# Five row groups of 256, 384, 512, 512 and 384 in place of four of 512, and a shorter free run of gathers, in a recommendation tower

## Chip, core and metric

The kernel runs on one core of one Trainium2 chip. The metric is the device time of one execution in microseconds (us). Engines are named as the profile names them: PE is TensorE (PEld its weight loads), DVE is VectorE, ACT is ScalarE, POOL is GpSimd, SP is SyncE, which here only issues DMAs.

## What is computed

2,048 rows, 40 table fields, embeddings of 64 values. Each row gathers 40 embeddings by index. For each of the 780 field pairs (i, j) with i < j a 64 x 64 matrix W is applied to embedding i and the result is multiplied with embedding j and summed. The 780 sums and 16 dense values go through three dense layers (512, 256, 1).

```python
e = jnp.stack([tbl_0[ids[:, 0]], ..., tbl_39[ids[:, 39]]], axis=1)
viW = jnp.einsum('bpd,pde->bpe', e[:, i_idx, :], W)
z = jnp.einsum('bpe,bpe->bp', viW, e[:, j_idx, :])
h = jnp.concatenate([z, dense_ctx], axis=1)
h = jnp.maximum(h @ W_top1 + b_top1, 0.0)
h = jnp.maximum(h @ W_top2 + b_top2, 0.0)
y = h @ W_top3
```

All values are fp32.

## The kernel before

The 2,048 rows are worked on in groups (`SIZES`, four of 512). A group has 128-row tiles (`TILES`, four each). The 40 fields form 20 pairs; pair m of a group (m = 0 to 19) holds fields 2(19 - m) and 2(19 - m) + 1, so the highest fields come first.

**Gathers (POOL, L459).** One indirect DMA fetches one field for one tile of 128 rows, so a pair takes 2 x TILES gathers: 8 in every group, 160 a group, 640 in all. The first four pairs of a group go to `VN` (two buffers, by group), the other sixteen to a ring `stage` of four pairs. Before pair m POOL waits until the pair four places before it in the ring has been transposed (L445, `tr_before`), and before the first pair of group g > 1 until group g - 2 is through the multiplies (L444). In group 0 the gathers run freely behind each other; from pair `RUN_PAIRS` = 4 on, every second tile is preceded by a "rest", a memset of a scratch tile (L456) that POOL waits for. In groups 1 to 3 each gather has a mark, computed ahead by `schedule`: it waits for a given count of PE steps (L451), or, where the mark is None, does a rest.

**Units (PE, DVE, ACT).** A transpose step turns a pair around on PE (L606) and ACT copies it to `V` (L489). Row k of a group is the work of field pair k with all higher ones; it needs pair m = 19 - k and those before it, so rows run from k = 19 down to 0. A group has 136 "a" and "d" units, whose matmuls (L624) stream the group's rows (512 columns), and B_ROWS x TILES = 64 "b" units, whose matmuls (L620) stream 512 columns of weights for one tile of 128 rows, whatever the group's size. Every unit has 16 matmul instructions and one DVE multiply (L564 for a and d, L555 for b). Two a or d units share one reduction step on PE (L644, 16 matmuls, 68 steps a group, streaming the group's rows). The b products are summed by ACT (L477, 16 pairs of instructions a unit) or, for some units, by DVE (L539). At the end of a group come one transpose step of those sums (L653), two passes over `z` (L494, L573, L501, L507) and seven MLP steps (L665 four times, L672 twice, L678), which are spread over the next group's units; those of the last group stand at its end.

**Order.** PE, ACT and DVE follow orders computed before the kernel is built. `schedule` keeps a clock of its own (`now`, `STEP_US`, `GATHER_US`, `REST_US`, `LAND_US`) to order the transposes among the steps and to place the gather marks: one gather each time its variable `due` has passed, and `due` then moves on by `SPACE_US`.

**Weights (SP, L430).** W is loaded in chunks of 640 KB into three slots, 22 chunks a group, in each group again.

Of the kernel before, what the change touches and what calls it, by code (L numbers as in the profile page):

```python
# [5 lines left out]
B, F, D, DENSE = 2048, 40, 64, 16  # L6
N1, N2 = 512, 256
P128 = 128
SIZES = (512, 512, 512, 512)
GROUPS = len(SIZES)  # L10
GB = max(SIZES)
FIRST_ROW = [sum(SIZES[:_g]) for _g in range(GROUPS)]
TILES = [_s // P128 for _s in SIZES]
PAIRS = F // 2
JP = 4
J0 = PAIRS - JP
CROWD = 11
# [4 lines left out]
def row_items(k):  # L22

    last = J0 if k < B_ROWS else PAIRS
    out = [("b", k)] if k < B_ROWS else []
    out += [("a", k, jp) for jp in range(last - 1, k, -1)]
    return out + ([("d", k)] if k % 2 == 0 else [])  # L30


def group_units(g):

    a_items = [item for k in reversed(range(PAIRS)) for item in row_items(k) if item[0] != "b"]
    b_items = [("b", k, t) for k in reversed(range(B_ROWS)) for t in range(TILES[g])]
    out, i, last = [], 0, 0  # L40
    for a, item in enumerate(a_items):
        out.append(item)
        coming = a_items[a + 1][1] if a + 1 < len(a_items) else -1
        while i < len(b_items):
            k = b_items[i][1]
            if g == 0 and not (k >= item[1] or k > coming):
                break
            if a < (3 + 1.94 * i if g else last if k >= CROWD else last + 2):
                break
            out.append(b_items[i])  # L50
            i, last = i + 1, a
    return out
# [4 lines left out]
UNITS = [(_g, _u) for _g in range(GROUPS) for _u in GROUP_UNITS[_g]]  # L57
# [111 lines left out]
def gathers(m):  # L169


    return 2 * TILES[m // PAIRS]
# [16 lines left out]
               if x % PAIRS >= JP and (stage_index(m) - stage_index(x)) % STAGE_SLOTS == 0)  # L189


RUN_PAIRS = 4
MLP_APART = 24


def red_at(q):


    late = 1.9 if q % QUADS == PART_ENDS[0] else 0
    return min(A_AT[2 * q + 1] + LAG + 0.1 + late, TOTAL - 0.4 + 0.0001 * q)  # L200


def ztr_at(g):


    return B_AT[B0[g + 1] - 1] + 7.2


def mlp_at(g, m):


    at = red_at((g + 1) * QUADS - 1)
    return at + 0.01 * (m + 1) if g == GROUPS - 1 else int(at) + 12.6 + MLP_APART * m


def pair_needed(step):


    return step[1] * PAIRS + PAIRS - 1 - UNITS[step[2]][1][1]


def tr_before(m):


    before = stage_index(m) - STAGE_SLOTS
    if m % PAIRS < JP or before < 0:
        return 0
    return before // (PAIRS - JP) * PAIRS + before % (PAIRS - JP) + JP + 1


def stage_free(m, transposed):
    return transposed >= tr_before(m) and (m % PAIRS or m < 2 * PAIRS or transposed >= 0)


STEP_US = {"main": 0.885, "red": 0.885, "tr": 0.65, "ztr": 1.0}
GATHER_US, REST_US, LAND_US, SPACE_US = 1.25, 0.55, 6.0, 1.6


def step_us(step):
    if step[0] == "mlp":  # L240
        return 6.15 if step[2] < 4 else 3.6 if step[2] < 6 else 1.8
    return STEP_US[step[0]]


def schedule():

    steps = [(n, ("main", UNITS[n][0], n)) for n in range(TOTAL)]  # L250
    steps += [(red_at(q), ("red", *divmod(q, QUADS))) for q in range(GROUPS * QUADS)]
    steps += [(ztr_at(g), ("ztr", g, 0)) for g in range(GROUPS)]
    steps += [(mlp_at(g, m), ("mlp", g, m)) for g in range(GROUPS) for m in range(MLP_STEPS)]
    steps = [s for _, s in sorted(steps, key=lambda x: x[0])]
    landed, end = {}, 8.0
    for m in range(PAIRS):
        end += gathers(m) * GATHER_US + (TILES[0] // 2 * REST_US if m >= RUN_PAIRS else 0)
        landed[m] = end + 2.2
    out, marks, count, now, due, pair = [], [], {"main": 0, "red": 0, "mlp": 0, "ztr": 0}, 0.0, end, 0
    issued = PAIRS  # L260
    for at, step in enumerate(steps):
        if step[0] == "main":
            need = pair_needed(step)
            while pair <= need:
                now = max(now, landed[pair]) + STEP_US["tr"] + (1.3 if pair == need else 0)
                out.append(("tr", *divmod(pair, PAIRS)))
                pair += 1
        if pair < issued and landed[pair] <= now and (pair < 2 * PAIRS or count["main"] >= U0[pair // PAIRS - 1] + 4):
            out.append(("tr", *divmod(pair, PAIRS)))
            now += STEP_US["tr"]  # L270
            pair += 1
        out.append(step)
        now += step_us(step)
        count[step[0]] += 1
        room = int(step_us(steps[at + 1]) / 1.9) if at + 1 < len(steps) else 0
        if due > now + (0.9 if room > 1 else 0):
            continue
        for extra in range(max(room, 1)):
            if issued == GROUPS * PAIRS or step[0] == "ztr" or not stage_free(issued, pair):
                break  # L280
            marks.append(None if extra else (step[0], count[step[0]]))
            if extra + 1 >= room:
                due = max(now + 1.9 * extra - 1.0, due) + SPACE_US
            if len(marks) == sum(gathers(m) for m in range(PAIRS, issued + 1)):
                landed[issued] = now + 1.9 * extra + LAND_US
                issued += 1
    return out, marks
# [30 lines left out]
def z0_tile(g):  # L318


    return ZT if g % 2 else 0
# [6 lines left out]
def build(nc, ids, tables, dense_t, w_units, w1, b1, w2, b2, w3, y):  # L328
# [6 lines left out]
    with ctx:  # L335
        def sb(name, shape, dt=fp32):
            return ctx.enter_context(nc.sbuf_tensor(name, shape, dt))
# [18 lines left out]
        idx = sb("idx", [P128, B // P128, F], i32)  # L356
        ident = sb("ident", [P128, P128])
        sel = sb("sel", [P128, 63])
        rest = sb("rest", [P128, 256])

        Ups = ctx.enter_context(nc.psum_tensor("Ups", [P128, U_SLOTS, 2, 512], fp32))
        Zps = ctx.enter_context(nc.psum_tensor("Zps", [P128, 2, 512], fp32))
# [29 lines left out]
        def wait(eng, s, value):  # L392
            if value > 0:
                eng.wait_ge(s, value)

        def natural_rows(m, t):


            g, r = divmod(m, PAIRS)
            if r < JP:  # L400
                at = P128 * (JP - 1 - r)
                return VN[:, g % 2, t, at:at + P128]
            return stage[:, stage_index(m) % STAGE_SLOTS, t, :]

        def landed(m):
            r = m % PAIRS
            return natural[r] if r < JP else gathered[stage_index(m) % STAGE_SLOTS]

        @block.sync
        def _(sp):  # L410
            sp.dma_start(idx[:, :, :], ids).then_inc(idx_loaded, 16)
            for c, (group, load) in enumerate(CHUNKS):
# [11 lines left out]
                for g in range(GROUPS):  # L424
                    if c == w_of(J_LAST[g])[0] + 4:
                        sp.wait_ge(z0_done, g + 1)
                        sp.dma_start(z[DENSE_ROW:DENSE_ROW + DENSE, z0_tile(g), :SIZES[g]],
                                     dense_t[:, FIRST_ROW[g]:FIRST_ROW[g] + SIZES[g]]).then_inc(dense_loaded, 16)
                x = W_SETS[min(group, 1)] + load
# [4 lines left out]
        @block.gpsimd  # L434
        def _(pool):
            pool.memset(ident[:, :], 0.0).then_inc(ident_zeroed, 1)
            pool.wait_ge(ident_zeroed, 1)
            pool.affine_select(out=ident[:, :], in_=ident[:, :], compare_op=ALU.not_equal, fill=1.0, base=0,
                               pattern=[[-1, P128]], channel_multiplier=1).then_inc(ident_ready, 1)
            pool.wait_ge(idx_loaded, 16)  # L440
            pool.wait_ge(ident_ready, 1)
            marks, rests = iter(GATHER_MARKS), 0
            for m in range(GROUPS * PAIRS):
                g, r = divmod(m, PAIRS)  # L444
                if r == 0 and g > 1:  # L445
                    pool.wait_ge(mul_done, U0[g - 1])
                wait(pool, tr_done, tr_before(m))
                for t in range(TILES[g]):
                    for f in range(2):
                        mark = next(marks) if g else None  # L450
                        if mark:  # L451
                            kind, count = mark
                            pool.wait_ge({"main": main_done, "red": red_done, "mlp": mlp_done}[kind], count)
                        elif g or m >= RUN_PAIRS and f == 0 and t % 2 == 0:
                            rests += 1
                            pool.memset(rest[:, :], 0.0).then_inc(rested, 1)  # L456
                            pool.wait_ge(rested, rests)
                        field = 2 * (PAIRS - 1 - r) + f
                        pool.indirect_dma_start(  # L459
                            out=natural_rows(m, t)[:, D * f:D * f + D], out_offset=None, in_=tables[field][:, :],  # L460
                            in_offset=bass.IndirectOffsetOnAxis(
                                ap=idx[:, FIRST_ROW[g] // P128 + t, field:field + 1], axis=0),
                        ).then_inc(landed(m), 16)
# [272 lines left out]
```

## Time and profile before

| | us |
|---|---|
| Median of 3 runs | 1421.53 (1421.38 to 1423.5) |
| Profiled execution, its own time | 1418.47 |
| Profiled execution, span | 1416.7 |
| PE busy | 1265.5 (89%) |
| DVE busy | 989.6 (70%) |
| ACT busy | 880.7 (62%) |
| POOL busy | 624.0 (44%) |
| DMA, mean over 16 engines | 60 GB/s |

The span runs from the first to the last instruction of the profiled execution; the execution's own time is 1.8 us longer. An engine's busy time is the union of its instructions' times. In the windows below "(x647)" is the number of instructions that began in the window; for POOL that counts gathers and rests together.

### The profile page before, as it was taken

The page shows a single profiled execution, that of the slowest core. Times are in us where ns is not written, and L with a number is a line of the kernel's source. Part 1 is how long each engine was busy: PE and PEld are TensorE (multiplying, and loading weights), DVE is VectorE, ACT ScalarE, POOL GpSimd, SP SyncE. Part 2 cuts the span into 40 slices and gives each one's busy share as a digit, 9 for nine tenths or more (in the row PEclk, how much of TensorE's full clock was granted, in tenths as well). Part 3 has the DMA queues.
Part 4 walks back from the last instruction along what each step waited for, and adds up shares of the span by engine and source line. Part 5 has one row for each costly group of instructions (what it writes and reads, how often), then busy time and mean ns, then how long its engine had stood idle before and what let it go on. Part 6 is the DMA issues. An engine that isn't in the chain of part 4 may idle for free.

```text
span 1416.7 us, 46045 instructions
## 1 busy us (share of the span) xinstructions
PE 1265.5 (89%) x17808; PEld 483.8 (34%) x17808; DVE 989.6 (70%) x855; ACT 880.7 (62%) x6749; POOL 624.0 (44%) x700
## 2 busy tenths in 40 slices
PE   1027788999999999999999999999999999999999
PEld 0011122233343443333333434343334333333333
DVE  0024554557898787778888777878888777799990
ACT  0004444546756387668786577778875677788871
POOL 6735344431355555555555555555555555100000
PEclk9998889999999999999999999999999999999999
DMA  4102111111222222222222222222232122212200
GB/s 154 25 16 54 32 53 34 52 50 45 69 59 77 76 62 57 75 56 77 57 76 68 68 77 58 75 51 68 71 79 77 39 78 57 65 40 60 75 21 0
DMA packets 34752, 84.45 MB, mean 60 GB/s; under 512 B 12196, under 2 KB 12708, under 8 KB 34408
## 3 DMA queue, kind: packets, MB, share of 16 engines
q1 hardware_dynamic: 14048, 60.50, 13.9%
q0 software_dynamic: 20480, 21.01, 7.5%
q8 instruction: 142, 2.33, 0.7%
q14 instruction: 74, 0.61, 0.1%
q10 hardware_dynamic: 8, 0.01, 0.0%
HBM read 81.47 MB, written 0.01 MB: 58 GB/s over the span
## 4 chain that ended last, share of the span: by engine, by line
PE 68%; issue 10%; DVE 9%; another core or an unknown queue 8%; ACT 4%; DVEq 0%
PE Ups L624 29%; PE Ups L620 14%; PE Zps L644 13%; PE Ups L665 7%; DVE P L564 6%; ACT PB L477 3%; DVE PB L555 2%; PE Ups L672 2%; PE Ups L606 2%; DVE zB L539 1%; PE Ups L678 0%; PE Ups L653 0%; ACT V L489 0%; ACT L489 0%
## 5 line engine op out<-in xcount | busy, mean ns | idle before, releaser
L477 ACT ACTIVATE PB<-PB 128x64 f32<-128x64 f32 x3312 | 798.7, 250 | 257.9 <-DVE PB L555 223.4
L564 DVE TENSOR_TENSOR P<-Ups,V 128x1024 f32<-128x1024 f32 x544 | 650.7, 1220 | 276.9 <-remote 153.1
L624 PE MATMUL Ups<-V,wf 64*32 64x512 f32 x8704 | 661.3, 602 | 100.9 <-ACT V L489 63.9
L477 ACT ACTIVATION_READ_ACCUMULATOR PB<-PB 128x1 f32 x3312 | 648.0, 196 | 0.5 <-issue 0.5
L459 POOL DMA_INDIRECT stage<-tbl,idx x512 | 484.6, 947 | 345.0 <-PE Ups L624 161.1
L555 DVE TENSOR_TENSOR PB<-Ups,VN 128x1024 f32<-128x1024 f32 x256 | 311.8, 1220 | 113.1 <-PE Ups L620 64.2
L620 PE MATMUL Ups<-wf,V 64*32 64x512 f32 x4096 | 347.5, 607 | 14.2 <-issue 6.6
L644 PE MATMUL Zps<-P,sel 64*32 64x512 f32 x4352 | 342.2, 596 | 2.0 <-issue 1.1
L624 PEld LDWEIGHTS Ups<-V,wf 64*32 64x32 f32 x8704 | 191.1, 107 | 420.1 <-issue 189.7
L459 POOL DMA_INDIRECT VN<-tbl,idx x128 | 121.2, 947 | 133.8 <-PE Ups L624 78.3
L620 PEld LDWEIGHTS Ups<-wf,V 64*32 64x32 f32 x4096 | 98.6, 108 | 181.9 <-issue 116.3
L644 PEld LDWEIGHTS Zps<-P,sel 64*32 64x32 f32 x4352 | 111.1, 108 | 144.4 <-issue 132.3
L489 ACT COPY V<-Ups 128x512 f32<-128x512 f32 x80 | 46.1, 576 | 134.9 <-remote 66.5
L665 PE MATMUL Ups<-z,w1s 128*128 128x512 f32 x224 | 99.6, 598 | 0.0
L456 POOL MEMSET rest<- 128x256 f32 x54 | 17.6, 325 | 112.1 <-PE Ups L606 112.1
L665 PEld LDWEIGHTS Ups<-z,w1s 128*128 128x128 f32 x224 | 41.5, 190 | 58.2 <-issue 50.5
L539 DVE TENSOR_REDUCE zB<-PB 128x16 f32<-128x1024 f32 x49 | 59.3, 1210 | 0.0
L515 ACT ACTIVATE h<-Ups,b1s 128x512 f32<-128x512 f32 x16 | 11.0, 689 | 77.0 <-PE Ups L665 77.0
L606 PEld LDWEIGHTS Ups<-ident,stage 128*128 128x128 f32 x256 | 27.9, 142 | 54.8 <-issue 23.0
L606 PE MATMUL Ups<-ident,stage 128*128 128x128 f32 x256 | 42.7, 290 | 2.1 <-DVE P L564 1.0
L606 PE MATMUL Ups<-ident,VN 128*128 128x128 f32 x64 | 11.8, 312 | 29.2 <-DMA VN<-tbl,idx 28.9
L672 PE MATMUL Ups<-h,w2s 128*128 128x512 f32 x64 | 29.2, 602 | 0.6 <-DVE P L564 0.6
(21 smaller groups left out, 63.0 us busy)
## 6 DMA issues: line engine op xcount, KB each, us to landing
wf<-w_units SPq DMA_DIRECT2D x88, 640.0 KB
stage<-tbl,idx POOLq DMA_INDIRECT x512
VN<-tbl,idx POOLq DMA_INDIRECT x128
w1s<-w SPq DMA_DIRECT2D x1, 1792.0 KB
w2s<-w SPq DMA_DIRECT2D x1, 512.0 KB
idx<-ids SPq DMA_DIRECT2D x1, 320.0 KB, 3.0
z<-dense_t SPq DMA_DIRECT2D x4, 32.0 KB
y<-z ACTq DMA_DIRECT2D x4, 2.0 KB
```

The costliest lines, as they stand in the source:

```text
L459: pool.indirect_dma_start(out=natural_rows(m, t)[:, D * f:D * f + D], out_offset=None, in_=tables[field][:, :], in_offset=bass.IndirectOff ...
L477: last = act.activation(p, p, ACT.Copy, accum_out=zB[:, t, at:at + 1])
L489: act.copy(V[:, v_slot(g, PAIRS - 1 - x), :rows], Ups[:, slot, 0, :rows]).then_inc(v_done, 1)
L539: dve.tensor_reduce(zB[:, t, at:at + 4 * JP], PB[:, i % PB_SLOTS, :, :].rearrange("p b (j e) -> p (b j) e", e=D), AX.X, ALU.add).then_inc( ...
L555: dve.tensor_tensor(PB[:, B_INDEX[n] % PB_SLOTS, :, :], Ups[:, slot, :, :], v, ALU.mult).then_inc(mul_done, 1)
L564: dve.tensor_tensor(P[:, A_INDEX[n] % P_SLOTS, :, :rows], Ups[:, slot, :, :rows], v, ALU.mult).then_inc(mul_done, 1)
L606: last = pe.transpose(Ups[:, slot, 0, P128 * t:P128 * (t + 1)], natural_rows(m, t), ident[:, :])
L620: last = pe.matmul(Ups[out, slot, b, :], V[rows, v_slot(g, k), r0:r0 + 32], wf[rows, c % W_SLOTS, at:at + WB_COLS], start=True, stop=True)
L624: last = pe.matmul(Ups[out, slot, b, :size], wf[rows, c % W_SLOTS, at + 32 * strip:at + 32 * strip + 32], V[rows, v_slot(g, field), :size] ...
L644: last = pe.matmul(Zps[out, h, :size], sel[rows, 31 - to:63 - to], P[rows, a % P_SLOTS, strip % 2, :size], start=at == 0, stop=x + 1 == PA ...
L665: last = pe.matmul(Ups[:, slot, 0, :size], w1s[:, k % ZT, P128 * x:P128 * (x + 1)], z[:, k, :size], start=n == 0, stop=n == ZT - 1)
L672: last = pe.matmul(Ups[:, slot, 0, :size], w2s[:, k, P128 * (x - 4):P128 * (x - 3)], h1[:, k, :size], start=k == 0, stop=k == 3)
```

## The change

The group sizes become 256, 384, 512, 512 and 384, so `TILES` is 2, 3, 4, 4, 3 and the groups have 4, 6, 8, 8 and 6 gathers a pair. A matmul of an a or d unit, of a reduction, a transpose copy and an MLP step then streams 256 or 384 columns in the smaller groups; a b unit stays as it is, and there are 16 x TILES of them. In group 0 only the first 14 pairs (56 gathers) are issued in the free run, with one rest before each pair from the fifth on (`QUIET_PAIRS` = 4); its last six pairs (24 gathers) and all of groups 1 to 4 have marks. The rest tile has 512 columns in place of 256. The spacing between marks becomes 1.4, 1.4, 1.5, 1.6 and 1.7 us of the schedule's clock, by group. The b units of groups 1 to 4 are spread evenly over the a units for any number of them. W is read five times.

```diff
-SIZES = (512, 512, 512, 512)
+SIZES = (256, 384, 512, 512, 384)
...
-            if a < (3 + 1.94 * i if g else last if k >= CROWD else last + 2):
+            if a < (3 + 124 * i / len(b_items) if g else last if k >= CROWD else last + 2):
...
-RUN_PAIRS = 4
+RUN_PAIRS, QUIET_PAIRS = 14, 4
...
-GATHER_US, REST_US, LAND_US, SPACE_US = 1.25, 0.55, 6.0, 1.6
+GATHER_US, REST_US, LAND_US = 1.25, 0.6, 6.0
+SPACE_US = (1.4, 1.4, 1.5, 1.6, 1.7)
...
     if step[0] == "mlp":
-        return 6.15 if step[2] < 4 else 3.6 if step[2] < 6 else 1.8
-    return STEP_US[step[0]]
+        return (6.15 if step[2] < 4 else 3.6 if step[2] < 6 else 1.8) * SIZES[step[1]] / GB
+    if step[0] == "main":
+        return STEP_US["main"] * (1 if step[1] == "b" else SIZES[UNITS[step[2]][0]] / GB)
+    return STEP_US[step[0]] * SIZES[step[1]] / GB
...
-    for m in range(PAIRS):
-        end += gathers(m) * GATHER_US + (TILES[0] // 2 * REST_US if m >= RUN_PAIRS else 0)
+    for m in range(RUN_PAIRS):
+        end += gathers(m) * GATHER_US + (REST_US if m >= QUIET_PAIRS else 0)
         landed[m] = end + 2.2
...
-    issued = PAIRS
+    issued = RUN_PAIRS
...
             while pair <= need:
+                while pair not in landed:
+                    marks.append(None)
+                    due = max(due, now) + GATHER_US + REST_US
+                    if len(marks) == sum(gathers(m) for m in range(RUN_PAIRS, issued + 1)):
+                        landed[issued] = due + LAND_US
+                        issued += 1
                 now = max(now, landed[pair]) + STEP_US["tr"] + (1.3 if pair == need else 0)
...
-                due = max(now + 1.9 * extra - 1.0, due) + SPACE_US
-            if len(marks) == sum(gathers(m) for m in range(PAIRS, issued + 1)):
+                due = max(now + 1.9 * extra - 1.0, due) + SPACE_US[issued // PAIRS]
+            if len(marks) == sum(gathers(m) for m in range(RUN_PAIRS, issued + 1)):
...
-        rest = sb("rest", [P128, 256])
+        rest = sb("rest", [P128, 512])
...
-                        mark = next(marks) if g else None
+                        mark = next(marks) if m >= RUN_PAIRS else None
...
-                        elif g or m >= RUN_PAIRS and f == 0 and t % 2 == 0:
+                        elif m >= RUN_PAIRS or m >= QUIET_PAIRS and (t, f) == (0, 0):
```

## Rows read from the trace of the kernel before

**Rows 1.** Timeline from the start (start us, us, engine, line, operation, idle before).

```profile
3.98 1.10 POOL L459 DMA_INDIRECT VN<-tbl,idx  x1 [2.50 <-DMA idx<-ids]
...
43.84 0.33 POOL L456 MEMSET rest<- 128x256 f32 x1
44.45 0.95 POOL L459 DMA_INDIRECT stage<-tbl,idx  x1 [0.27 <-issue]
...
50.92 1.22 DVE L564 TENSOR_TENSOR P<-Ups,V 128x1024 f32<-128x1024 f32 x1 [49.86 <-remote]
...
85.33 0.95 POOL L459 DMA_INDIRECT stage<-tbl,idx  x1 [0.30 <-issue]
92.92 1.22 DVE L564 TENSOR_TENSOR P<-Ups,V 128x1024 f32<-128x1024 f32 x1 [40.78 <-remote]
93.67 0.59 ACT L489 COPY V<-Ups 128x512 f32<-128x512 f32 x1 [66.54 <-remote]
...
94.40 3.49 PE L624 MATMUL Ups<-V,wf 64*32 64x512 f32 x32 [57.81 <-ACT V L489]
```

**Rows 2.** Windows, one for each of the first three groups.

```profile
core 0: us, PE busy (x) PEld busy (x) DVE busy (x) ACT busy (x) POOL busy (x), PEclk, DMA share, GB/s
94.00:474.00 380.00, 339.53 (x4408) 118.78 (x4410) 253.91 (x219) 199.25 (x1532) 157.29 (x182) 0.95 0.20 53
474.00:783.00 309.00, 301.28 (x4479) 119.10 (x4465) 246.72 (x213) 224.88 (x1729) 167.22 (x182) 1.00 0.26 68
783.00:1093.00 310.00, 301.37 (x4464) 125.47 (x4452) 246.19 (x212) 225.49 (x1728) 167.23 (x182) 1.00 0.26 67
```

**Rows 3.** Windows: free gathers, none, marked ones, none (columns as in group 2).

```profile
205.00:330.00 125.00, 112.09 (x1158) 36.90 (x1165) 66.45 (x57) 60.47 (x475) 49.33 (x60) 0.95 0.16 41
330.00:367.00 37.00, 36.52 (x647) 13.46 (x639) 34.75 (x31) 32.62 (x255) 0.00 (x0) 1.00 0.19 56
420.00:460.00 40.00, 39.62 (x676) 15.92 (x669) 36.02 (x31) 26.75 (x211) 21.75 (x23) 1.00 0.27 71
1340.00:1375.00 35.00, 34.82 (x648) 11.66 (x632) 35.00 (x32) 31.86 (x265) 0.00 (x0) 1.00 0.18 56
```

**Rows 4.** Timeline of one burst of eight gathers in group 0.

```profile
205.90 2.35 DVE L564 TENSOR_TENSOR P<-Ups,V 128x1024 f32<-128x1024 f32 x2 [2.47 <-remote]
...
212.44 0.95 POOL L459 DMA_INDIRECT stage<-tbl,idx  x1 [0.27 <-POOL rest L456]
...
221.51 0.95 POOL L459 DMA_INDIRECT stage<-tbl,idx  x1 [0.31 <-issue]
...
223.87 1.23 DVE L564 TENSOR_TENSOR P<-Ups,V 128x1024 f32<-128x1024 f32 x1 [8.91 <-remote]
...
214.43 4.29 PE L620 MATMUL Ups<-wf,V 64*32 64x512 f32 x13
```

**Rows 5.** The chain of waits at the end (start us, us, what).

```profile
1381.60 24.23 PE Ups L665 x56
1405.83 6.87 PE Ups L672 x16
1412.69 1.82 PE Ups L678 x4
```

**Rows 6.** Groups of instructions by line (xcount | busy us, mean ns).

```profile
L555 DVE TENSOR_TENSOR PB<-Ups,VN 128x1024 f32<-128x1024 f32 x256 | 311.8, 1220 | 113.1 <-PE Ups L620 64.2 <-remote 19.7 <-PE Ups L624 17.8
L539 DVE TENSOR_REDUCE zB<-PB 128x16 f32<-128x1024 f32 x49 | 59.3, 1210 | 0.0
L573 DVE TENSOR_TENSOR z<-Zps,z 128x512 f32<-128x512 f32 x4 | 2.7, 682 | 0.0
L436 POOL MEMSET ident<- 128x128 f32 x1 | 0.2, 205 | 0.3 <-POOLq L728 0.3
```

**Rows 7.** Timeline of a marked gather in group 1.

```profile
664.92 0.94 POOL L459 DMA_INDIRECT VN<-tbl,idx  x1 [0.80 <-PE Ups L624]
```

**Rows 8.** Timeline of weight loads on PE, one half step.

```profile
338.53 0.15 PEld L624 LDWEIGHTS Ups<-V,wf 64*32 64x32 f32 x8 [0.28 <-issue]
```

**Rows 9.** The DMA queue of the weight chunks (packets, MB, share).

```profile
q1 hardware_dynamic: 14048, 60.50, 13.9%
```

## Prediction

> **What bounds the kernel now.** I read the windows by group first, then windows around the bursts of group 0, then the timeline of the start and the chain's end. Unless said otherwise, instructions are PE matmuls counted in a window.
>
> A group issues 200 x 16 + 68 x 16 + 20 x 4 + 8 = 4,376 PE matmuls without its MLP, which the windows bear out (4,408 in the stretch of group 0; 4,479 and 4,464 in those of groups 1 and 2, with 76 of an MLP each) [rows 2]. Where no gather runs, PE needs 37 / 647 = 57.2 ns for one (35 / 648 = 54.0 in the other such window) [rows 3]. A group is thus 250.3 us of PE, and an MLP 24.2 + 6.9 + 1.8 = 32.9 us [rows 5]. Groups 1 and 2 need 309 and 310 us against 284: the rest, 24 and 26 us, I lay on their marked gathers, some 175 each (182 POOL instructions less rests) [rows 2], so 0.145 us a gather.
>
> Group 0 is another matter. Its window takes 380 us for 4,408 x 0.0572 = 252 us of work [rows 2]. The 182 POOL instructions there are 96 free gathers with 24 rests and 62 marked ones. Marked ones cost 62 x 0.145 = 9, so 119 us are left over 96 free gathers: 1.24 us each. The window with bursts alone says the same: 48 gathers and 12 rests, 125 - 1,158 x 0.0572 = 59 us, 1.22 a gather [rows 3]. The burst shows it: gathers run from 212.4 to 222.5, PE issues 13 matmuls over 4.3 us from 214.4 and DVE's next multiply comes at 223.9, after 8.9 us of waiting for nothing that the profile names [rows 4]. Gathers 1.25 us apart, with 0.3 us between them, stop the other engines; marked ones with 0.8 us between [rows 7] hardly do. The start is the same stop made longest. Gathers run from 3.98 to 86.3; ACT's third copy, whose transposes are long done, comes at 93.67 after 66.5 us, and PE goes on at 94.4, 8.1 us after the last gather [rows 1].
>
> The parts give 94.4 + 250.3 + 119 + 9 for group 0, 3 x (250.3 + 32.9) for groups 1 to 3 with the MLPs before them, 418 x 0.145 = 61 for their gathers, and 35.1 for the end from 1381.6: 1,418 against a span of 1,416.7. The account closes, so I change its terms one by one.
>
> **The start.** POOL stops when the ring is full, after pair 7: 64 gathers before, 32 after. The last begins at 3.98 and ends after 32 x 1.25 = 40.0 us, plus four rests. A rest of 256 columns took 0.33 and added 0.3 (0.33 and 0.27 in place of one gap of 0.3) [rows 1]; 128 columns took 0.205 [rows 6], so 512 should take 0.57 and add 0.54, 2.2 in all. Last gather ended 46, PE goes on 8.1 later: 54 in place of 94.4. If PE gets its few early steps done, no later than this; if the 0.57 us rests let it through, some us earlier.
>
> **Group 0 on PE.** Exactly half of every column count: 125.2. The trace has no matmul of 256 columns with 64 x 32 weights. From below, the step halves and nothing is added. From above, a step costs what it costs at 512, 0.86: 204 steps (136 + 68) x 0.43 = 87 more. Nearer is the lower end, since eight weight loads took 0.15 us of a half step of 0.43 [rows 8], which leaves them inside 0.21. DVE sets a floor of its own: 136 multiplies of 512 elements at 0.682, 32 of 1,024 at 1.22, 9 row sums at 1.21 and one add, 143.4; two multiplies in a row took 2.35 in place of 2.44 [rows 4], and with only 1.13 from start to start it is 133. PE and DVE with nearly equal loads and three PSUM slots won't mesh fully: I take 138, 13 over PE's own.
>
> The rule of the Trainium skill (TensorE: Matmul & The Clock Gate, section LDWEIGHTS) is that a load takes its columns over 1.2 GHz, 26.7 ns for 32, so 16 loads would need 427 ns, the whole of a halved step. By it, as an estimate, the step is neither longer nor has it slack. The trace's 0.15 us for eight disagrees on the busy time; no row shows them at this rate for long.
>
> **Free gathers against work.** Pairs 8 to 13, 24 gathers, are free while PE has work: 24 x 1.24 = 30. Each waits for a transpose, in bursts of four with a rest; PE held out 2 us into the burst before it stopped [rows 4], so 15 is the low end. I keep 30. The other 72 of the 96 that cost 1.24 are gone.
>
> **Marked gathers.** By the diff's clock the run ends at 8 + 56 x 1.25 + 10 x 0.6 = 84. Rows 11 to 7 of group 0 go as their pairs land, row 6 starts about 91 and the group ends near 165, so 81 / 1.4 = 58 marks fall into it: 24 of its own and 34 of group 1. In group 0 that is 58 x 0.145 = 8, in groups 1 to 4 the other 526 x 0.145 = 76. They are closer together now: 1.4 of the planned clock, some 1.6 to 1.65 real (1.6 planned was about 1.77 real: 309 / 175), a gap of 0.7 in place of 0.8. Between 0.145 at 0.8 and 1.24 at 0.3 no row stands. If the cost fell in a straight line, the 178 marks at 1.4 would cost 0.17 more each and the 160 at 1.5 0.10 more, 46 us; if it jumps somewhere below 0.7, nothing. A mark waits for PE, so delay thins the gathers out by itself; I take 15.
>
> **Groups 1 to 4.** 1,792 of 2,048 rows: 7/8 x 4 x 250.3 = 876. The MLPs of groups 0 to 3 stream 1,664 rows: 3.25 x 32.9 = 107. Steps of 384 columns leave eight loads 0.32 us, nothing added; DVE's op of 768 elements lies halfway, 0.95, beside 0.96 of PE for an a unit with its half reduction.
>
> **Supply of group 1.** Here a new wait comes: 34 of 120 gathers are in when it starts, pair m is complete (6(m + 1) - 34) x 1.4 + 6 later, and PE, at some 1.45 us an a unit with its share of b units and MLP plus 0.5 a transpose, wants pairs 8 to 10 at 27, 34 and 43 against 34, 42 and 51. PE waits about 9 us. Later groups start with half or more of theirs in.
>
> **Weights.** 22 more chunks. 60.5 MB took 13.9% of 1,417, 197 us of all 16 DMA engines [rows 9], so 2.1 us a chunk; group 0 needs one each 8 us. SP's queue holds only these and the dense rows. Cost nothing; without the three slots it would be 2.1 a chunk.
>
> **The end.** The last MLP has 384 columns: 24.7 and 2.2 behind it, 26.9 in place of 35.1.
>
> **Sum.** Group 0: 54 + 125.2 + 13 + 30 + 8 = 230.2. Then 876 + 107 + 76 + 15 + 9 + 26.9 = 1,109.9. Span 1,340; the execution's own time 1.8 more, and the median of the runs 3.1 above the profiled one: 1,345, 5.4% less than 1,421.5.
>
> **Rivals.**
>
> 1. The stop isn't cured by fewer gathers. Something else ends it, and PE goes on near 94 as before: 1,345 + 40 = 1,385. For it: the releaser has no name. Against it: group 0 shows the stop ending with the burst each time. The Trainium skill (SBUF — State Buffer, Who interferes with whom) has only DVE and GpSimd share a port and says ACT never waits for one; by that the gathers would not hold ACT's copy at all, and this rival would be the case. The trace differs: ACT too waited 66.5 us [rows 1].
>
> 2. Closer marks cost as on the straight line, or more: 46 in place of 15, up to 80: 1,376 to 1,410.
>
> 3. Group 1 starves. If the ring or the late PE keeps the 34 gathers out, pair 10 comes 34 x 1.4 = 48 us later: 1,345 + 45 = 1,390.
>
> 4. Slower than before: PE's short steps don't shrink. At full length they cost 87 in group 0 and 2 x 204 x 0.21 = 87 in the two groups of 384, 175 less the 13 counted: 1,507. It decides from where a 256-column step costs 0.43 + (76 + 13) / 408 = 0.65 us. For it: such steps carry 16 loads and 16 matmuls each. Against it: the loads fill a third of PE's time now (11.66 of 35) [rows 3].
>
> 5. The head start is given back in full, since PE is at work nearly all the time from 94 on: no change, 1,421. Against it: PE's 89% busy hides group 0, where 380 us held 252.
>
> **Chances.** My sum 0.62; rival 1 0.07; rival 2 0.12; rival 3 0.09; rival 4 0.07; rival 5 0.03. Within 0.2% is what a measurement of this kernel can't tell from none. Faster: the first four, 0.90; the same 0.02 of rival 5; slower 0.08. Low end: no step or mesh cost (-13), free gathers 15, marks and supply nothing (-24): 1,293. High end: rivals 1 to 3 up to 1,395, where rival 4 and the worst of rival 2 are left out. The sum's own range is 1,315 to 1,370.
>
> **What the profile after would show.** PE goes on at 54 us (rival 1: near 90). Group 0 through its last reduction near 230. Reductions of 256 columns 0.43 to 0.5 us apart where PE isn't waiting (rival 4: over 0.65). POOL's last gather some 1.6 us after the one before in groups 0 and 1, and the loss a gather there near 0.2. PE waits for transposed pairs only in the first half of group 1, under 25 us. The groups of 512 take 300 to 312. The last MLP is 24.7 long. I'd be wrong most easily in the price of a gather between 0.3 and 0.8 us of gap, and in how DVE and PE mesh in group 0.

## The result, and the profile after

The changed kernel takes 1,426.3 us (median of 17 runs) where the kernel before takes 1,420.7 in as many: ratio 1.0046, 95% interval 1.0035 to 1.0057. 5.4% less was forecast; it is 0.46% slower. Two further comparisons gave 1.0027 (1.0011 to 1.0042) and 1.0038 (1.0022 to 1.0054). One of the ten executions of the changed kernel in the first of the two took 3,122 us; it is left out of that ratio, and no trace shows why.

The windows of the kernel after, one for the start and one for each group, in the columns of [rows 2]:

```profile
0.00:45.00 45.00, 3.93 (x38) 1.62 (x38) 1.55 (x4) 2.29 (x4) 32.32 (x42) 1.00 0.38 125
45.00:244.00 199.00, 172.29 (x3842) 89.92 (x3842) 136.67 (x178) 97.89 (x761) 80.47 (x88) 0.94 0.31 86
244.00:532.00 288.00, 251.65 (x4187) 124.69 (x4190) 189.81 (x194) 171.66 (x1313) 136.03 (x146) 0.94 0.26 69
532.00:860.00 328.00, 305.41 (x4464) 122.94 (x4456) 246.08 (x213) 223.85 (x1729) 168.40 (x182) 0.98 0.24 64
860.00:1169.00 309.00, 299.56 (x4473) 116.34 (x4465) 245.46 (x212) 227.93 (x1763) 163.49 (x177) 1.00 0.26 68
1169.00:1397.00 228.00, 223.52 (x4098) 94.37 (x4087) 183.46 (x192) 165.03 (x1299) 39.89 (x44) 1.00 0.22 64
```

Against the forecast's own terms (its 15 us for closer marks are shared out here as 7 and 6, with rounding):

| stretch | forecast us | measured us |
|---|---|---|
| start | 54 | 45 |
| rest of group 0 (256 rows) | 176 | 199 |
| group 1 (384), 142 gathers | 187.7 + 16.5 + 21 + 9 + 7 = 241 | 288 |
| group 2 (512), 177 gathers | 250.3 + 24.7 + 26 + 6 = 307 | 328 |
| group 3 (512) | 250.3 + 32.9 + 25 = 308 | 309 |
| group 4 (384) | 187.7 + 32.9 + 6 = 227 | 228 |
| end | 26.9 | 27.6 |

The last three agree to 1 us each. The head start is there and 9 us larger than forecast. All of the loss against the forecast, some 90 us (23, 47 and 21), lies in groups 0 to 2.

The start in the timeline, which answers to [rows 1]: ACT's third copy now comes at 44.7, while POOL still gathers, and PE goes on at 45.3.

```profile
18.84 0.37 ACT L498 COPY V<-Ups 128x256 f32<-128x256 f32 x1 [3.75 <-PE Ups L615]
...
40.40 0.54 POOL L465 MEMSET rest<- 128x512 f32 x1
...
44.74 0.37 ACT L498 COPY V<-Ups 128x256 f32<-128x256 f32 x1 [25.53 <-issue]
...
45.26 1.96 PE L633 MATMUL Ups<-V,wf 64*32 64x256 f32 x32 [23.32 <-issue]
```

POOL's first marked gather and, further on, a stretch of group 1 (POOL and PE rows of the timeline of the kernel after):

```profile
129.58 0.94 POOL L468 DMA_INDIRECT stage<-tbl,idx  x1 [25.63 <-PE Ups L633]
...
274.33 0.95 POOL L468 DMA_INDIRECT stage<-tbl,idx  x1 [0.27 <-POOL rest L465]
275.28 0.54 POOL L465 MEMSET rest<- 128x512 f32 x1
276.09 0.95 POOL L468 DMA_INDIRECT stage<-tbl,idx  x1 [0.27 <-POOL rest L465]
282.53 0.94 POOL L468 DMA_INDIRECT stage<-tbl,idx  x1 [5.49 <-PE Ups L633]
283.78 0.94 POOL L468 DMA_INDIRECT stage<-tbl,idx  x1 [0.30 <-issue]
...
278.63 0.87 PE L615 MATMUL Ups<-ident,stage 128*128 128x128 f32 x3 [6.56 <-DMA stage<-tbl,idx]
280.17 1.54 PE L633 MATMUL Ups<-V,wf 64*32 64x384 f32 x16 [0.66 <-ACT V L498]
```

Two things are to be seen. POOL, free after the last free gather, stood 25.6 us for its first mark, since the mark counts PE's steps and PE was behind the clock by which marks were placed. And in group 1 PE waited 6.6 us for a pair; POOL, its unmarked gathers done at 277, then waited 5.5 us for the PE step after that pair. Each waits for the other in turn. Over the whole of group 1 (244 to 532) PE waits 26.4 us for pairs, and its granted clock is 0.94:

```profile
PE Ups L615 <- DMA stage<-tbl,idx: 26.4, 6, 6.6
```

The worst stretch is 250 to 350. PE is busy 68.55 of 100 us there, at a mean granted clock of 0.83: behind some of the waits it runs at the lower of its two levels, 1.2 in place of 2.4 GHz.

```profile
250.00:350.00 100.00, 68.55 (x1004) 32.59 (x987) 45.87 (x48) 42.14 (x320) 40.94 (x46) 0.83 0.19 48
105.00:129.50 24.50, 21.31 (x570) 11.10 (x574) 20.68 (x27) 19.65 (x159) 0.00 (x0) 1.00 0.25 70
```

The second row is the stretch of POOL's idle time in group 0: no gather is issued there. Its matmuls, grouped by line:

```profile
L633 PE MATMUL Ups<-V,wf 64*32 64x256 f32 x308 | 13.0, 382 | 3.1 <-ACT V L498 2.6 <-DVE PB L564 0.5
L653 PE MATMUL Zps<-P,sel 64*32 64x256 f32 x160 | 6.9, 377 | 0.0
L629 PE MATMUL Ups<-wf,V 64*32 64x512 f32 x96 | 6.5, 595 | 0.2
L615 PE MATMUL Ups<-ident,stage 128*128 128x128 f32 x6 | 1.3, 300 | 0.0
```

Here and below I weigh PE's work by the pace of full steps before: 53.6 ns for a matmul of 512 columns and half for 256, 162.5 ns for a transpose (the planner's 0.65 us for four; in the trace before, four take 0.59, so this is a little high, alike for all sizes), and an MLP's by its 32.9 us for 512 rows; what a stretch takes beyond that is its loss. By this weighing the whole kernel is 1,108 us of PE work, with either set of sizes. These four lines are 468 x 26.8 + 96 x 53.6 + 6 x 162.5 ns = 18.7 us of work in 24.5. The single steps show where the rest doesn't go:

```profile
118.76 0.67 PE L633 MATMUL Ups<-V,wf 64*32 64x256 f32 x16 [1.05 <-ACT V L498]
119.19 0.67 PE L653 MATMUL Zps<-P,sel 64*32 64x256 f32 x16
119.62 1.10 PE L629 MATMUL Ups<-wf,V 64*32 64x512 f32 x16
120.47 0.67 PE L633 MATMUL Ups<-V,wf 64*32 64x256 f32 x16
```

From start to start a step of 256 columns takes 0.43 us (118.76, 119.19, 119.62), exactly half of what one of 512 takes (0.86; 119.62 to 120.47 is 0.85). So a small step by itself costs no more than its share; the loss lies in waits between steps. 3.1 us are idle time of PE, 2.6 of them for ACT's copy of a pair that was transposed just before.

### The profile page after: what moved, and what is told of

Its sections match the earlier page's. It is cut to its first block, busy times and chain, and to the rows that moved or that the text cites. A ratio compares the mean times of both kernels' runs of the same rounds, so it can differ in the third digit from the quotient of the medians.

```text
span 1424.6 us, 53364 instructions
## 1 busy us (share of the span) xinstructions
PE 1281.9 (90%) x21148; PEld 563.6 (40%) x21148; DVE 1003.0 (70%) x989; ACT 893.4 (63%) x6876; POOL 620.6 (44%) x676
## 4 chain that ended last, share of the span: by engine, by line
PE 73%; DVE 9%; issue 7%; ACT 5%; another core or an unknown queue 3%; DMA 2%; POOL 0%; DVEq 0%; ACTq 0%
PE Ups L633 31%; PE Ups L629 15%; PE Zps L653 14%; PE Ups L674 7%; ACT PB L486 5%; DVE P L573 4%; DVE PB L564 3%; PE Ups L615 2%; PE Ups L681 2%; DMA stage<-tbl,idx 2%; DVE zB L548 1%; ACT V L498 1%; PE Ups L687 0%; PE Ups L662 0%
## 5 line engine op out<-in xcount | busy, mean ns | idle before, releaser
L573 DVE TENSOR_TENSOR P<-Ups,V 128x1024 f32<-128x1024 f32 (+2 forms) x680 | 665.7, 1004 | 281.5 <-PE Ups L633 212.4
L633 PE MATMUL Ups<-V,wf 64*32 64x384 f32 (+2 forms) x10880 | 685.5, 519 | 72.0 <-issue 27.7
L486 ACT ACTIVATION_READ_ACCUMULATOR PB<-PB 128x1 f32 x3360 | 633.9, 189 | 0.0
L633 PEld LDWEIGHTS Ups<-V,wf 64*32 64x32 f32 x10880 | 236.1, 107 | 383.3 <-issue 196.4
L653 PE MATMUL Zps<-P,sel 64*32 64x384 f32 (+2 forms) x5440 | 369.3, 510 | 1.2 <-DVE P L573 0.5
L629 PE MATMUL Ups<-wf,V 64*32 64x512 f32 x4096 | 326.0, 611 | 7.4 <-DVE P L573 4.8
L653 PEld LDWEIGHTS Zps<-P,sel 64*32 64x32 f32 x5440 | 140.6, 108 | 131.5 <-issue 107.9
L498 ACT COPY V<-Ups 128x384 f32<-128x384 f32 (+2 forms) x100 | 48.8, 488 | 117.1 <-PE Ups L615 77.7
L674 PE MATMUL Ups<-z,w1s 128*128 128x384 f32 (+2 forms) x280 | 102.9, 522 | 0.2 <-DVE PB L564 0.2
L681 PE MATMUL Ups<-h,w2s 128*128 128x384 f32 (+2 forms) x80 | 30.0, 520 | 1.1 <-DVE P L573 1.1
```

The costliest lines, as they stand in the source:

```text
L486: last = act.activation(p, p, ACT.Copy, accum_out=zB[:, t, at:at + 1])
L498: act.copy(V[:, v_slot(g, PAIRS - 1 - x), :rows], Ups[:, slot, 0, :rows]).then_inc(v_done, 1)
L573: dve.tensor_tensor(P[:, A_INDEX[n] % P_SLOTS, :, :rows], Ups[:, slot, :, :rows], v, ALU.mult).then_inc(mul_done, 1)
L629: last = pe.matmul(Ups[out, slot, b, :], V[rows, v_slot(g, k), r0:r0 + 32], wf[rows, c % W_SLOTS, at:at + WB_COLS], start=True, stop=True)
L633: last = pe.matmul(Ups[out, slot, b, :size], wf[rows, c % W_SLOTS, at + 32 * strip:at + 32 * strip + 32], V[rows, v_slot(g, field), :size] ...
L653: last = pe.matmul(Zps[out, h, :size], sel[rows, 31 - to:63 - to], P[rows, a % P_SLOTS, strip % 2, :size], start=at == 0, stop=x + 1 == PA ...
```

## The experiments

Three theories. *Supply*: gathers come too late, because marks hold POOL to PE's steps while PE waits for pairs. *Sizes*: small groups cost more than their share of columns. *Spacing*: gathers closer together disturb the engines more. The "lead" below is the number of gathers issued beyond a group's end; before, it was 62, 76 and 90 at the ends of groups 0 to 2, after, 33, 55 and 72.

Kernels run together share a chip and its runs of the kernel before. That kernel took 1,431, 1,434 and 1,432 us in three such sets, on three chips, and 1,229.6 and 1,229.8 in two others, both on one and the same fourth chip. Below, these are the 1,430 kind and the 1,230 kind. Whole times are compared as ratios within a set; stretches are compared within a kind.

**rests_g01** and **rests_g01_again.** Marks of groups 0 and 1 replaced by rests:

```diff
                         mark = next(marks) if m >= RUN_PAIRS else None
+                        if g < 2:
+                            mark = None
```

> The changed kernel, but the gathers of group 0 after the free run and of group 1 have no marks: each has a rest (the 512-column memset) ahead of it and otherwise runs as the ring allows. Supply theory (the marks hold POOL to PE's clock: it idled 25.6 us in group 0 and some 5.5 us after each late pair of group 1, while PE then waits for pairs): POOL takes 1.76 us a gather without idling, the waits of PE for pairs in groups 1 and 2 go, 1,424 falls by 45 to 70 to some 1,355 to 1,380. Column theory (steps of 256 and 384 columns cost PE more than their share): within 10 us of 1,424. Spacing theory (gathers planned 1.4 apart disturb the engines more): 10 to 25 less.

> The changed kernel with rests and no marks in groups 0 and 1. It was 1.9% faster than the kernel before on the 1,431 chip. On a chip of the 1,420 kind: the same, about 2% below the kernel before and 2% to 2.5% below the changed kernel of this call. On the other kind: 10 to 25 us below the changed kernel, since only PE's waits for pairs go, and still slower than before.

Measured: 1,403.8 beside 1,431.4, ratio 0.9809 (0.9792 to 0.9825) to the kernel before, and again 1,404.8, ratio 0.9795 (0.9768 to 0.9822). The changed kernel took 1,438.4 in that second set, so this is 34 us less than the change. Group 1 takes 248 us in place of 288 (291 in the second set), group 0 some 10 more. Lead at the end of group 0 is 48. PE's waits for pairs (who waited for whom, PE alone, whole kernel; us, times, longest) in the kernel after and in this one:

```profile
PE Ups L615 <- DMA stage<-tbl,idx: 36.0, 9, 6.6
```

```profile
PE Ups L617 <- DMA stage<-tbl,idx: 9.7, 3, 4.9
```

In group 1 itself PE waits for no pair any more and the clock is granted at 1.00. Of the 41 us that group 1 gives back, 26 are the waits; how the rest divides between the clock and gathers that crowd less (see below) no run parts. Supply is shown as the main loss of group 1, but 34 is below the 45 to 70 expected: group 2, which starts with a lead of 55 in both, keeps its 332 us (both kernels of the second set), some 9.6 of them waits for pairs.

**wide_marks.**

```diff
-SPACE_US = (1.4, 1.4, 1.5, 1.6, 1.7)
+SPACE_US = (1.8, 1.8, 1.5, 1.6, 1.7)
```

> The changed kernel with 1.8 in place of 1.4 as spacing of the marks in groups 0 and 1. Supply theory: the gathers come still later and PE waits more, 20 to 50 us slower. Spacing theory: 10 to 25 us faster. Column theory: no change within 5 us.

Measured: 1,506.9, ratio 1.0527 (1.0509 to 1.0544), some 70 us over the change, more than supply was expected to cost (20 to 50). Leads fall to 20 and 41; group 1 takes 320 and group 2 373. PE's waits for pairs, and its busy time from 246 to 346 us, 44 us at a granted clock of 0.67:

```profile
PE Ups L615 <- DMA stage<-tbl,idx: 97.0, 16, 10.6
```

```profile
246.00:346.00 100.00, 44.21 (x560) 19.54 (x544) 26.10 (x27) 23.98 (x169) 49.18 (x62) 0.67 0.14 34
```

**sizes_free_g0.** The kernel before with

```diff
-SIZES = (512, 512, 512, 512)
+SIZES = (256, 384, 512, 512, 384)
...
-            if a < (3 + 1.94 * i if g else last if k >= CROWD else last + 2):
+            if a < (3 + 124 * i / len(b_items) if g else last if k >= CROWD else last + 2):
```

> The kernel before with the five group sizes and the even spread of b units, nothing else: all 80 gathers of group 0 are free, the marks and their clock are as before (the clock counts a 256- or 384-column step as long as one of 512, so marks are placed closer in real time). Supply theory: group 0 loses 1.24 us for each of 48 gathers behind the start, but group 1 gets its gathers early: below the changed kernel, 1,370 to 1,410. Column theory: group 0 and the two groups of 384 lose as in the changed kernel, 1,425 or above. Spacing theory: marks closer than 1.4 in group 1 stop the engines, 1,440 or above.

Measured: 1,462.7, ratio 1.0227 (1.0209 to 1.0245). Group 0 ends at 316, with free gathers as before. Group 1 starts with a lead of 91 and PE waits 0.5 us for pairs in the whole kernel, yet the group takes 282.5 for 204 us of work at a granted clock of 1.00, with a gather each 1.72 us; in rests_g01 it took 248 with one each 1.95. So ample supply is not enough, and the supply theory's figure (1,370 to 1,410) was wrong.

The averages hide what differs. In the groups of the 1,430 kind that are compared here the median distance of two gathers is 1.72 to 1.76 us whatever the marks. Not so the number that come within 1.3 us of the one before, back to back: 43 of 164 in this group 1, 7 of 127 in that of rests_g01. Where a mark has passed already, POOL waits for nothing: the gather at 283.78 in the timeline above comes 0.30 us behind the one that was held up. So a closer mark isn't a slightly smaller gap each time, but more gathers at the gap of a burst. That this makes the loss fits here and in the next runs; no run varied it alone.

**marks_512, marks512_16, marks512_16_again.** The changed kernel with the sizes undone:

```diff
-SIZES = (256, 384, 512, 512, 384)
+SIZES = (512, 512, 512, 512)
-RUN_PAIRS, QUIET_PAIRS = 14, 4
+RUN_PAIRS, QUIET_PAIRS = 7, 4
-SPACE_US = (1.4, 1.4, 1.5, 1.6, 1.7)
+SPACE_US = (1.4, 1.4, 1.5, 1.6)
```

That is marks_512; the other two have `(1.4, 1.6, 1.6, 1.6)` in the last line.

> The changed kernel with four groups of 512: the free run is again 56 gathers (7 pairs of 8), the other 104 of group 0 have marks. Supply theory: marks at some 2.1 us a gather take 220 us for what bursts took 237 and the start is 14 us earlier: 1,395 to 1,425. Column theory: no small steps, so only the gain stays: 104 gathers at 0.15 in place of 1.24, 1,330 to 1,350. Spacing theory: 1,360 to 1,400.

> Four groups of 512 with the shortened free run and marks in group 0 at 1.4, all later marks at 1.6 as before. The run with closer marks lost 55 us in group 1 and 37 in group 2 where the kernel before lost 31 and 33. Spacing theory: those go back to 31 to 35 as long as the 69 gathers of lead at the end of group 0 suffice: 20 to 28 us less than with closer marks, some 3.5% to 4% below the kernel before. Supply theory: less lead, waits of PE in group 1 or 2, no gain.

> Four groups of 512, shortened free run, marks at 1.4 in group 0 and 1.6 after. It was 1.4% slower than the kernel before on the 1,230 chip. On a chip of the 1,420 kind: no bursts in group 0 and enough lead, 3% to 4% faster than before (1,370 to 1,385). On a chip of the other kind: again 1.4% slower.

Measured: marks_512 1,403.9 beside 1,431.4, 0.9807 (0.9790 to 0.9824), in the range that the supply theory gave. The change with its own marks but without its sizes thus gains 1.9%, and the change as it is loses 0.3% to 0.4% on this kind: the sizes together, head start included, cost over 2% where they were to gain. marks512_16_again 1,373.8 beside 1,433.8, 0.9582 (0.9557 to 0.9607), as expected. Group 1 takes 314 with marks at 1.6 and 333 with 1.4, although the closer marks gave the larger lead at its start (69 against 59), and PE waits for no pair in either: that is spacing, some 19 us over 174 and 190 gathers. Back to back come 20 of the 174 and 53 of the 190, so by this pair a gather back to back costs some 0.6 us (an estimate, 19 / 33). On the other kind of chip marks512_16 takes 1,246.1 beside 1,229.6, 1.0141: there it loses.

**last256.** Sizes 256, 512, 512, 512, 256, with the edit of rests_g01.

> Groups of 256, 512, 512, 512 and 256 rows, gathers of groups 0 and 1 with rests and no marks. Its last group has 256-column steps and runs without gathers. Column theory at 256: the last group with the MLP of the one before takes some 190 to 200 us where its share is 158, and DVE is busy near 90%. If the small steps are slow only beside gathers: 160 to 170. As a whole: group 1 of 512 rows starts with under 50 of its 160 gathers in and PE waits 30 to 40 us, so within 1% of the kernel before, either way.

It ran on the other kind of chip: 1,295.2 beside 1,229.6, 1.0540. Group 1 starts with a lead of 40 and takes 328; PE waits 31.8 us for pairs in all, as expected, but the whole was expected within 1% of the kernel before. Its last group, free of gathers, takes 165 for 146 us of weighed work, a loss of 12% of its time at a granted clock of 1.00:

```profile
1107.00:1270.00 163.00, 157.09 (x3696) 79.20 (x3688) 123.43 (x168) 111.52 (x874) 0.00 (x0) 1.00 0.28 83
```

A gather-free stretch of 512 rows, in the windows of marks512_16 on the same chip, loses 1.3 of 40 us, some 3%:

```profile
1120.00:1160.00 40.00, 39.48 (x644) 13.14 (x636) 34.97 (x32) 35.63 (x290) 0.00 (x0) 1.00 0.18 52
```

DVE isn't the bound in the group of 256 (123 of 163). In the last group 256 columns thus cost some 15 us over what 512 lose, about what the forecast put (13 us), well below the 190 to 200 expected here. A quarter of the time is lost only in group 0, which differs in two ways: its b units follow its rows two at a time in place of being spread, and its pairs are transposed just before their use.

**half_before, half_after, and both again.** One gather for both fields of a pair, and a rest in place of every mark. Both kernels leave out the right embeddings: every gather reads the same table by the same ids, so the sums are others and only the time is of use.

```diff
-                    for f in range(2):
...
+                    for f in range(1):
+                        if m >= 4:
+                            rests += 1
...
-                            out=natural_rows(m, t)[:, D * f:D * f + D], out_offset=None, in_=tables[field][:, :],
+                            out=natural_rows(m, t), out_offset=None,
+                            in_=tables[3].rearrange("(v two) d -> v (two d)", two=2),
...
-                                ap=idx[:, FIRST_ROW[g] // P128 + t, field:field + 1], axis=0),
+                                ap=idx[:, FIRST_ROW[g] // P128 + t, 1:2], axis=0),
```

> The kernel before with half as many gathers: one indirect DMA fetches 128 values a row for both fields of a pair (from table 3, two rows as one, by the ids of field 1, so the sums are of other embeddings), each after the first 16 has a rest of 512 columns ahead, none has a mark. PE's order is unchanged. Supply is thus ample for either grouping. Start near 45 to 54, no bursts: 1,220 to 1,250.

> The changed kernel with the same halved, unmarked gathers (same change of the computation). Only the group sizes still differ from the kernel beside it. If supply was all that the change lost to, the smaller first group now brings its start (some 15 to 20 us) and the shorter last MLP (8): 1,200 to 1,215, 20 to 30 below the other. If 256-column steps also cost a quarter more than their share, as the gather-free window of 24.5 us in group 0 with 18.4 us of work says, that takes 20 to 30 back and the two are within 10 us.

> The kernel before with halved, unmarked gathers (all after the first 16 with a rest; sums of other embeddings), on a chip where gathers stop the engines if this call gets one. There the first stop ends with the gathers that fill the ring, PE goes on at 50 to 55 us; then gathers at 1.76 us cost 0.15 each: 1,225 to 1,245. On the other kind again 1,202.

> The changed kernel with the same gathers. On the other kind of chip it was 40 us slower than its partner although supply was ample. If sizes alone cost that (first rows of each group wait for a transpose and its copy, and 256-column steps mesh badly), it is 25 to 45 us slower here too, the start being worth 15 to 20 more. If the loss of the change on this kind of chip is supply alone, it is 15 to 25 us faster than its partner.

Both pairs ran on the 1,230 kind of chip: 1,202.5 and 1,242.7, then 1,203.4 and 1,242.4. PE waits for no pair of the ring in any of the four. With ample supply the new sizes cost 40 us; the expected gain or tie is refuted. The weighed work is the same in both (1,108 us); in the first 120 us half_before loses 50.9 and half_after 49.3, and from there on 42.5 and 83.8. By groups the whole losses are 57, 12, 12 and 10 in the four of half_before, and 62, 22, 20, 13 and 14 in the five of half_after. So the sizes cost something by themselves, in groups of 512 behind smaller ones too, that no term of the forecast had but the 13. Its cause is open, and no such pair ran on the 1,430 kind.

**short_run512, short_run512_again, short_after.** `RUN_PAIRS = 4` in marks512_16 and in the changed kernel.

> Four groups of 512, free run of 4 pairs (32 gathers), all others marked, 1.4 in group 0 and 1.6 after. With a run of 7 pairs POOL stood from 75 to 119 us and PE began at 83. Here the run ends at 44, PE goes on near 52 and the marks keep coming: 20 to 30 us less than with 7 pairs, so 5.5% to 6.5% below the kernel before on a chip of the 1,430 kind. Rival: the marked gathers of pairs 4 to 10 can't be ahead of PE's small early rows and PE waits for each, within 10 us of the 7-pair version (4.2% below).

> The changed kernel with a free run of 4 pairs (16 gathers) in place of 14 (56). The first stop ends near 31 in place of 45 us and 24 gathers no longer stop PE, against 40 more gathers tied to PE's steps in the poorest stretch of supply. Supply theory: leads at the ends of groups 0 and 1 stay at 33 and 55 or fall, so groups 1 and 2 lose as much as in the changed kernel, and PE waits in group 0 too: within 1.5% of the changed kernel. If the free gathers were what the change lost: 30 or more faster.

> Four groups of 512 with a free run of 4 pairs. It was 3.5% slower than the kernel before on the 1,230 chip, where the run of 7 pairs was 1.4% slower, so marks from pair 4 on cost 27 us of supply there. On a chip of the 1,430 kind the earlier end of the stop gives 20 to 30 us and the supply takes 20 to 30: within 1% of the 7-pair version, 3.2% to 5.2% below the kernel before.

On the 1,230 kind: 1,272.8 (1.0352) and 1,339.4 (1.0897). The second has no partner there, so what it expected of the changed kernel stays untested. On the 1,430 kind short_run512_again takes 1,370.5, 0.9580 (0.9559 to 0.9602), where the run of 7 pairs had 0.9582: its rival was right. PE goes on at 49.4 in place of 83.4 us, but its waits for pairs rise from 15.9 to 44.7 us and use up most of it: the free run brings in pairs that PE's short early rows need at once, while marked gathers come only as PE gets on.

**before_again, after_again, after_third.** Unchanged kernels, for traces and ratios on one chip.

> The kernel before, unchanged, for its trace on this call's chip. The kernel before took 1,421 us where the change was measured and 1,431 and 1,230 in the two calls of experiments: the chips differ. If this chip is of the 1,420 to 1,430 kind, ACT's third copy comes near 94 us, after the gathers; if it is of the 1,230 kind, it comes within 1 us of its transposes at 36.5, and group 0 ends near 340 and not at 474.

> The changed kernel, unchanged. On a chip of the 1,420 kind: within 1% of the kernel before, as measured. On a chip where gathers stop nothing the change has only its costs and no stalls to remove: start 15 to 20 us earlier, last MLP 8 shorter, against waits of PE for pairs in groups 1 and 2 and the mesh at 256 columns: 2% to 5% slower, 1,255 to 1,290.

> The changed kernel once more. Where gathers stop the engines it is 0.3% to 0.5% slower than the kernel before. On the 1,230 kind of chip it has not been timed: there is no stop at the start and no burst cost to save, while the waits of PE for pairs and the 40 us that the halved pair shows for the sizes stay: 3% to 7% slower, 1,265 to 1,315.

1,433.0, 1,438.4 and 1,437.9, all on the 1,430 kind. before_again shows the same start as [rows 1] (third copy at 93.5). The changed kernel itself was never timed on the 1,230 kind; that part stays open.

## Why the prediction was wrong

**Right.** The start in the main (54 forecast, 45 measured), groups 3 and 4, the end, and that a step of 256 columns takes half of one of 512 (0.43 us). The lead of 34 gathers at the start of group 1 (33 measured) is right by its making, since marks tie gathers to counts of PE steps and not to time. That PE goes on before the run of gathers ends was put as possible "if the 0.57 us rests let it through"; that is not shown. In the seven traces of the 1,430 kind, or of the chip of the result, that start with 256 rows, ACT's third copy comes between 34.6 and 48.4 us, also with rests of 256 columns (sizes_free_g0, 40.1), while the starts with 64 or 56 free gathers of 512 rows have it 6.7 to 7.4 us behind the run each time.

**Wrong: "Supply of group 1".** The forecast took 1.4 us a gather, the planner's clock, although it had put the real pace at 1.6 to 1.65 two paragraphs before, and let it run on while PE waits. In the trace group 1 got 142 gathers in 288 us, 2.03 each, since a wait of PE becomes a wait of POOL. The term was 9 us; PE waited 26.4, and rests_g01, which cuts the tie, takes 41 out of group 1. Rival 3 named the place, at a price of 45, but made it hang on the 34 gathers staying out; they came, and it starved all the same.

**Wrong: "Later groups start with half or more of theirs in".** Group 2 starts with 55 of 160. Groups of 512 took 309 with leads of 62 to 90, 328 to 332 with 55, and 373 with 41. Some 20 us of the loss is here, 9.5 of them waits for pairs.

**Mis-sized: "Group 0 on PE".** 13 us over PE's share. In its gather-free stretch group 0 lost 5.8 us on 18.7 of work, which over the 126 us of its work would be 39 (an estimate from 24.5 us). That DVE sets it was argued and isn't shown: DVE was busy 20.7 of 24.5 us there, 84%. The steps themselves cost their share (0.43 us), and last256 has the cost near the forecast in a group whose b units are spread and whose pairs are all transposed before it begins. So what remains is the order of units in group 0, or that each of its pairs is transposed and copied right before use (2.6 of the 5.8 us); no run parts the two.

**Mis-sized: the price of a burst, 1.24 us a gather.** It was all that group 0 took beyond PE's pace, but for 9 us. These are the windows of group 0, from PE's going on to its end, in before_again and in marks512_16_again, on one chip:

```profile
94.00:484.00 390.00, 348.01 (x4408) 119.35 (x4411) 253.84 (x219) 199.29 (x1532) 157.22 (x182) 0.93 0.20 52
83.00:425.00 342.00, 299.33 (x4404) 117.93 (x4404) 254.45 (x219) 199.18 (x1531) 156.99 (x169) 0.93 0.23 60
```

By the forecast's prices, marks on 96 gathers that were free should save 96 x (1.24 - 0.145) = 105 us; they save 48. 15.9 us are new waits for pairs. The rest was not the bursts' alone: half_before has no burst and its group 0 still loses 57 us (on the other kind of chip). The change's sum used the price for 24 gathers only, and its group 0 doesn't tell this term from the one above. That the marks with 1.6 and the old sizes bring 4.2%, near the 5.4% forecast for the whole, is no proof of the sum: the change's own marks bring 1.9%.

**Mis-sized: the spacing term, 15.** marks_512 against marks512_16_again puts 1.4 in place of 1.6 at 19 us in one group of 512, where the straight line of rival 2 gives 190 x 0.17 = 32. Both took the gap for even, 0.8 us from one marked gather [rows 7]. It isn't: in groups 1 and 2 of the kernel before 15 of 173 and 17 of 174 marked gathers come within 1.3 us of the one before.

Rival 1 fell: PE went on at 45 us. Its ground was the port rule of the Trainium skill (SBUF — State Buffer, Who interferes with whom), by which gathers would not hold ACT's copy at all. The traces of the 1,430 kind differ from it: ACT's copy came 46 us after its transposes (marks512_16_again). On the 1,230 kind they agree: there the same instructions stop nothing. Rival 4 fell: it needed 0.65 us for a step of 256 columns, and where PE isn't kept waiting the steps are 0.43 apart, in group 0 and in last256's last group, where half of the 132 a and d steps begin 0.46 us or less before the next. Rival 5 described the result (head start given back) but not by its mechanism.

## What to carry to other kernels

Before making a first stage smaller, work out who supplies the second one: here marked gathers came one each 1.75 to 1.8 us in groups of 512, and such a group had to start with some 60 of its 160 in (59 were enough, with 55 PE waited). A wait of the supplier on the consumer's progress counter keeps bursts apart, but in a stretch where the consumer starves it turns every stall into one of the supplier; there a fixed pause costs less. And a planner's clock that runs ahead of the chip (1.4 planned, 2.0 real) must not be used as the chip's. Before calling a loss one of spacing, count the gathers that come back to back, and don't go by the mean.

## What was not expected of the hardware

The kernel before took 1,421 to 1,434 us in four sets of runs and 1,230 in two others on another chip, and the traces differ in what a row of gathers does to the other engines. The timeline of marks512_16 there, and of marks512_16_again on the 1,430 kind: transposes of the third pair at 35.4 in both, ACT's copy of them

```profile
35.39 1.09 PE L615 MATMUL Ups<-ident,VN 128*128 128x128 f32 x4 [4.59 <-DMA VN<-tbl,idx]
36.51 0.58 ACT L498 COPY V<-Ups 128x512 f32<-128x512 f32 x1 [9.41 <-PE Ups L615]
```

```profile
82.68 0.58 ACT L498 COPY V<-Ups 128x512 f32<-128x512 f32 x1 [55.67 <-remote]
```

POOL issues its gathers 1.25 us apart in both. On the first chip ACT copies at once; on the second, 46 us later, past the end of POOL's run at 75.3. Groups of 512 with an MLP and marks at 1.6 take 308 to 315 us on one kind and 288 to 292 on the other, some 0.12 us for each of their 174 gathers. Which resource is held, and what makes the chips differ, no run shows.
